# Token table of the second expert layer built sequence by sequence, and the first unit prepared norm first

## The chip, the cores and the metric

The kernel runs on one core of one Trainium2 chip. The metric is the time of one execution on the device in microseconds (us), taken as the median of several runs. Engines are named as in the profile: PE (matmuls), PEld (its weight loads), DVE (vector), ACT (scalar/activation), POOL (GpSimd), SP (the queue that issues most DMAs).

## The reference, cut to what matters

Two layers over `x` of shape (8, 256, 256): eight sequences of 256 tokens, width 256. Each layer is cross attention with 16 heads to a context of 256 tokens, added to `x`, and then a mixture of experts, added to `x`.

```python
x = x + tanh(g_xattn[0]) * L0_xattn(layernorm(x), ctx)      # layer 0
x = x + tanh(g_ffn[0])   * L0_ffn(layernorm(x))             # 8 experts (dense here) + a shared one
x = x + tanh(g_xattn[1]) * L1_xattn(layernorm(x), ctx)      # layer 1
x = x + tanh(g_ffn[1])   * L1_ffn(layernorm(x))             # 8 experts of 1024, each token to its top 2
# L1_ffn:
logits = x @ Wr + br;  mask = top-2 of the 8 logits;  w = softmax(logits where mask)
for e in range(8):
    out += (relu(x @ W1[e] + b1[e]) @ W2[e] + b2[e]) * (w * mask)[:, :, e]
```

## The kernel before, in words

**Units and slots.** A unit is one sequence of one layer: units 0 to 7 are layer 0, 8 to 15 layer 1. Every engine walks the same list of slots `PLAN` (made by `make_plan`), and in each slot it runs, in the order in which the list holds them, its own part of the stages named there. `base(u)` = 18 + 8u; a slot number here is a half step, so unit `u` starts its scores at slot 2*base(u). Waits between engines are semaphores; nothing reorders an engine's list at run time.

**Preparing a unit.** `ctx` turns the context (PE, then ACT), `kprod` makes the keys and `qprod` the queries (PE, then ACT writes a high part and DVE a low part), `stats`, `normal`, `turn` make the normed and turned `x` that `qprod` wants. SP stores keys and queries to DRAM and `load_stacks` brings them back stacked (`stack_k`, six DMAs; `stack_q`, six DMAs). `stats` is two steps on DVE (`bn_stats`, `bn_aggr`) and then eight tiny operations on POOL that make the inverse deviation `rstd` (L1702 to L1709). ACT then writes the normed rows (`normal`, L1020), PE turns them (`turn`, L655). For unit 0 the order is ctx, kprod, stats, normal, turn, qprod, stack.

**Scores.** `scores_by_query` (PE, L678) and `maxima` (DVE, L1243), `scores_by_key` (L699), exponentials on ACT, `weigh_values` (L714), `turn_values`, `attn_turn`, `project` (L741).

**Routing of layer 1.** For each sequence `b`, when its layer-1 attention is in: `pick_z` (DVE, and the add to `x` on POOL, L1724; for b = 7 on DVE), `stats` of ("finish", b), `normal`, `turn`, `logits1` (PE, L817; DVE ranks the eight logits and writes `mask` and `picks`), `soft1`, `count1` (PE: triangular and all-ones products of the masks, which give each token its place among the tokens of its expert), `weights1` (DVE, ending in L1475), a store of the rows, and `bias_turn` (L842) and `bias1` (L850), which add the expert bias and finish `x`. Before, `count1` writes into one array of all 16 tiles of tokens (`by_query`), and for b = 1 to 4 it stands at slots 294 to 297.

**After the last sequence.** `blocks` (DVE) turns the eight totals into 23 blocks of 256 slots, each of one expert. `tables` (DVE) then works on all 4096 picks at once: slot numbers, their tile and place, a 128x32x46 one-hot of the tile (`in_tile`, `in_tile_no`) and a 128x32x128 one-hot of the place (`at_place`, L1542, in four quarters); 32 matmuls (L881) make of them the token number of each slot, DVE makes `token_i` (L1589 to L1596). POOL gathers the rows by `token_i` (L1740), and the expert loop over the 23 blocks runs: `up` (L915), `down` (L931), scatter-add (L1753).

**What stands ahead of the expert loop.** PE: the b1 product (L888, after all eight `x` are finished), `turn_rows(0)` (L899), then `up(0)`. ACT: `split_w1(0)` (L1123), the copy `b1_all` (L1164), `split_w1(1)`, `split_rows(0)`. DVE: `split_w1(0)` (L1600), `split_w1(1)`, then `split_rows(0)` (L1611). SP: the store of the last rows, b1, then the first two blocks' W1 (`first_weights`).

Of the kernel before, what the change touches and what calls it, by code (L numbers as in the profile page):

```python
# [37 lines left out]
PICKS = TOPK1 * NT  # L38
# [22 lines left out]

def layer_of(u):
    return u // NB
# [11 lines left out]
def make_plan():  # L75

    at = defaultdict(list)
    for u in range(UNITS):
        g = 2 * base(u)
        at[g - 34].append(("load", u))  # L80
        at[g - 28].append(("ctx", u))
        at[g - 25].append(("kprod", u))
        at[g - 23].append(("stats", ("query", u)))
        at[g - 21].append(("normal", ("query", u)))
        at[g - 19].append(("turn", ("query", u)))
        at[g - 16].append(("qprod", u))
        at[g - 10].append(("stack", u))
# [9 lines left out]
    at[2 * base(0)].append(("out_bias", 0))  # L97
    at[2 * base(2)].append(("gate_turn", 0))
# [21 lines left out]
    for b in range(NB):  # L120
# [31 lines left out]
stats_done moments rstd rstd_chain norm_done turned xnT_ready  # L152
# [7 lines left out]
weights1_done rows_out0 rows_out1 rows_out2 rows_out3 biases_in b2_in table_chain in_tile_ready tile_no block_ready onehotT_ready b1_mm b1_ready  # L160
at_place_ready tokens_mm tokens_ready w1_in0 w1_in1 w2_in0 w2_in1 w1_hi w1_lo w2_hi w2_lo rows_in0 rows_in1 rows_in2 rows_in3 xs_turned
# [4 lines left out]
def bank_release(stage, n):  # L166

    if stage == "turn":
# [11 lines left out]
        "logits1": ("logits_ready", n + 1),  # L180
# [3 lines left out]
def share_banks():  # L184

    bank_of, uses = {}, []
    for g in sorted(PLAN):
        for stage, n in PLAN[g]:
            if stage in ("load", "stack", "stats", "normal", "take", "groups0", "ranks0", "weights0", "any_nan",
                         "reload", "load_alternative", "pick_z", "soft1", "count1", "weights1", "blocks", "tables") or (stage == "ctx" and layer_of(n)):  # L190
# [10 lines left out]
def build(nc, a, out):  # L201
# [40 lines left out]
    column_row = sb("column_row", [P, COLS])  # L242
# [4 lines left out]
    tile_start = sb("tile_start", [P, TOPK1 * NT])  # L247
    row_no = sb("row_no", [P, 1])
# [61 lines left out]

    b1 = sb("b1", [E1, H1])
# [3 lines left out]
    slots_all = sb("slots_all", [P, NT, E1])  # L315
    slots_pick = sb("slots_pick", [P, TOPK1, NT, E1])
    slot_f = sb("slot_f", [P, PICKS])
    slot_i = sb("slot_i", [P, 3, PICKS], I32)
    place_tile = sb("place_tile", [P, 2, PICKS])
    at_place = sb("at_place", [P, PICKS, P], BF16)  # L320
    in_tile = sb("in_tile", [P, PICKS, COLS])
    in_tile_no = sb("in_tile_no", [P, PICKS, 2, COLS], BF16)
# [6 lines left out]
    tok = sb("tok", [P, 3, COLS])  # L329
# [54 lines left out]
    def _(sp):  # L384
# [9 lines left out]
        def load_attention_weights(l):  # L394
            if l == 0:
                q_w, q_b, o_w, o_b = a["L0_xattn_q_w"], a["L0_xattn_q_b"], a["L0_xattn_proj_w"], a["L0_xattn_proj_b"]
                k_w, v_w = a["L0_xattn_kv_w"][:, 0:D], a["L0_xattn_kv_w"][:, D:2 * D]
                k_b, v_b = a["L0_xattn_kv_b"][0:D], a["L0_xattn_kv_b"][D:2 * D]
            else:
                q_w, q_b, o_w, o_b = a["L1_xattn_Wq"], a["L1_xattn_bq"], a["L1_xattn_Wo"], a["L1_xattn_bo"]  # L400
                k_w, v_w, k_b, v_b = a["L1_xattn_Wk"], a["L1_xattn_Wv"], a["L1_xattn_bk"], a["L1_xattn_bv"]
            for dst, src in (
                (wq[l][:, :, :], q_w.rearrange("(k p) n -> p k n", p=P)),
                (wkv[l][:, :, 0:D], k_w.rearrange("(k p) n -> p k n", p=CROWS)),
# [5 lines left out]
            for dst, col in ((qkb[l][:, 0, :], q_b), (qkb[l][:, 1, :], k_b), (vb[l][:, :], v_b)):  # L410
                sp.dma_start(dst, col.rearrange("(k p) -> p k", p=P),
                             allow_slow_non_contiguous=True).then_inc(attn_w_in[l], 16)
# [12 lines left out]
        def load_router():  # L425
            sp.dma_start(wr[:, :, :], a["L1_ffn_Wr"].rearrange("(k p) e -> p k e", p=P)).then_inc(sem.router_in, 16)
            sp.dma_start(br[:, :], a["L1_ffn_br"].partition_broadcast(P)).then_inc(sem.router_in, 16)
            sp.dma_start(b2[:, :], a["L1_ffn_b2"]).then_inc(sem.b2_in, 16)
# [50 lines left out]
        def load_stacks(u):  # L479
# [5 lines left out]
            for blk in range(PARTS):  # L485
                src = qk_dram[l][b, 2 + blk % 2].rearrange("(h two d) s -> two d h s", two=2, d=HD)
                for side in range(2):
                    o = HALF * side + blk * HD
                    sp.dma_start(stack_k[i][o:o + HD, :, :].bitcast(F32), src[side]).then_inc(k_in[i], 16)
            sp.wait_ge(sem.q_out, 32 * (u + 1))  # L490
# [74 lines left out]
        def store_rows(b):  # L565
            sp.wait_ge(sem.weights1_done, b + 1)
# [3 lines left out]
        sp.dma_start(g_raw[:, 0:2], a["g_xattn"].partition_broadcast(P)).then_inc(sem.gates_in, 16)  # L570
        sp.dma_start(g_raw[:, 2:4], a["g_ffn"].partition_broadcast(P)).then_inc(sem.gates_in, 16)
        load_x(0)
        load_ctx(0)
        stages = {"load": load, "ctx": context, "kprod": store_keys, "qprod": store_queries, "stack": load_stacks,
                  "shift_turn": place_shift, "mean_project": store_alternative, "project": store_z, "reload": reload, "load_alternative": load_alternative,
                  "weights1": store_rows, "bias1": store_x, "tables": first_weights}
# [17 lines left out]
    def _(pe):  # L594
# [215 lines left out]
        def logits1(b):  # L810
            no = NORM_NO["finish", b]
            bank = open_bank("logits1", b)
            pe.wait_ge(sem.router_in, 32)
# [7 lines left out]
        def count1(b):  # L821
# [954 lines left out]
```

## Time and profile before

| what | value |
|---|---|
| median of 3 runs | 1077.18 us (1073.37 to 1077.26) |
| the profiled execution's own time | 1083.7 us |
| its span, first to last instruction | 1081.9 us |
| PE busy | 943.0 us, 87% |
| DVE busy | 757.0 us, 70% |
| ACT busy | 479.5 us, 44% |
| POOL busy | 222.6 us, 21% |
| mean granted TensorE clock | 0.890 of full speed |
| expert loop, from the first `up` (792.65) to the end | 289.3 us |

The profiled execution is 6.5 us (0.6%) above the median of the timed ones. Shares of busy time are means over stages with different limits, so they are only a start: what a change in one stage is worth is read from the rows of that stage.

### The profile page before, as it was taken

The numbers are of one execution on the slowest core, as the hardware profiler recorded it, in microseconds if no ns is written. First come the engines' busy times: TensorE is split into PE (matmuls) and PEld (weight loads), VectorE is DVE, ScalarE is ACT, GpSimd is POOL, SyncE is SP. The second block draws the span as 40 slices with busy tenths as digits, with TensorE's granted clock in tenths as the row PEclk, the third lists the DMA queues.
The fourth block names the chain that finished last, engine by engine and source line by source line (L and its number), as shares of the span: only waits on it lengthen the run. The fifth ranks groups of instructions, "written<-read, shape, count | busy, mean of one in ns | idle before, by whom it ended". The sixth has DMA issues, their size and how long they took to land.

```text
span 1081.9 us, 17951 instructions
## 1 busy us (share of the span) xinstructions
PE 943.0 (87%) x6385; PEld 745.0 (69%) x6385; DVE 757.0 (70%) x1553; ACT 479.5 (44%) x834; POOL 222.6 (21%) x386
## 2 busy tenths in 40 slices
PE   3478899999999998899888868897479999999995
PEld 2345677777777665666655545564379999999995
DVE  2544475777676667788786688865668888888882
ACT  1115544344444442333423343442256667666762
POOL 2011210120201000000000012201044454445423
PEclk9756899999999998999989776655579999999998
DMA  4997563353262316366353873241257677667752
GB/s 117 203 224 151 108 124 61 52 106 69 50 100 54 62 61 110 87 109 139 83 108 94 157 202 96 87 122 42 108 197 243 197 231 235 217 202 233 236 152 29
DMA packets 121336, 142.16 MB, mean 131 GB/s; under 512 B 11456, under 2 KB 105560, under 8 KB 121120
## 3 DMA queue, kind: packets, MB, share of 16 engines
q1 hardware_dynamic: 112416, 128.77, 47.5%
q0 software_dynamic: 8832, 12.25, 5.2%
q8 instruction: 51, 0.84, 0.3%
q14 instruction: 37, 0.30, 0.1%
HBM read 109.97 MB, written 31.01 MB: 130 GB/s over the span
## 4 chain that ended last, share of the span: by engine, by line
PE 62%; DVE 20%; issue 7%; ACT 5%; DMA 3%; POOL 2%; SPq 1%; DVEq 0%; POOLq 0%; ACTq 0%
PE bank L931 12%; PE bank L770 7%; PE by_query L915 6%; PE by_key L915 6%; DVE rowmax L1243 5%; PE value_bank L714 4%; PE bank L780 4%; DVE clipped L1268 4%; PE bank L741 3%; PE by_query L678 3%; PE bank L634 3%; PE bank L625 3%; PE by_key L699 2%; PE bank L664 2%; DVE x L1398 1%
## 5 line engine op out<-in xcount | busy, mean ns | idle before, releaser
L1243 DVE TENSOR_REDUCE rowmax<-by_query 128x4 f32<-128x1024 f32 x128 | 155.7, 1217 | 26.6 <-PE by_query L678 26.4
L1057 ACT ACTIVATE probs<-clipped 128x1024 f32<-128x1024 f32 x64 | 67.6, 1057 | 183.7 <-DVE clipped L1268 183.7
L1702 POOL TENSOR_SCALAR rstd<-moments 128x2 f32<-128x2 f32 x32 | 7.1, 223 | 579.5 <-DVE moments L1207 579.5
L1753 POOL DMA_INDIRECT out_x<-x,token_i x46 | 78.2, 1700 | 146.5 <-ACT x L1158 139.5
L931 PE MATMUL bank<-w_hi,h_hi 128*128 128x256 f32 x368 | 104.1, 283 | 0.0
L931 PE MATMUL bank<-w_lo,h_hi 128*128 128x256 f32 x368 | 104.1, 283 | 0.0
L931 PE MATMUL bank<-w_hi,h_lo 128*128 128x256 f32 x368 | 104.1, 283 | 0.0
L678 PE MATMUL by_query<-stack_k,stack_q 48*128 48x256 f32 x512 | 70.9, 358 | 28.7 <-DVE rowmax L1243 23.2
L1268 DVE SCALAR_TENSOR_TENSOR clipped<-by_key,lower 128x512 f32<-128x512 f32 x128 | 82.0, 682 | 13.2 <-DMA lower<-max 11.1
L678 PEld LDWEIGHTS by_query<-stack_k,stack_q 48*128 48x128 f32 x512 | 43.2, 208 | 68.3 <-issue 35.5
L699 PE MATMUL by_key<-stack_q,stack_k 50*128 50x256 f32 x512 | 68.1, 348 | 19.6 <-DVE clipped L1268 15.6
L770 PE MATMUL bank<-xnT,w_gate 128*128 128x256 f32 x288 | 79.5, 399 | 5.5 <-DVE lo L1224 2.2
L780 PE MATMUL bank<-w_down,hidden 128*128 128x256 f32 x288 | 79.2, 398 | 4.6 <-DVE hidden L1384 1.5
L714 PE MATMUL value_bank<-probs,values 128*32 128x256 f32 x1024 | 80.4, 439 | 0.0
L699 PEld LDWEIGHTS by_key<-stack_q,stack_k 50*128 50x128 f32 x512 | 43.7, 209 | 48.3 <-issue 23.3
L770 PE MATMUL bank<-xnT,w_up 128*128 128x256 f32 x288 | 75.7, 386 | 0.0
L1398 DVE SCALAR_TENSOR_TENSOR x<-bank,expert_cols,x 128x256 f32<-128x256 f32 x144 | 62.5, 476 | 17.9 <-PE bank L780 17.8
L1090 ACT ACTIVATE act_gate<-bank 128x256 f32<-128x256 f32 x72 | 27.4, 380 | 103.8 <-PE bank L770 103.8
L1057 ACT ACTIVATE probs<-by_key 128x1024 f32<-128x1024 f32 x64 | 65.4, 1022 | 16.8 <-PE by_key L699 15.3
L931 PEld LDWEIGHTS bank<-w_hi,h_hi 128*128 128x128 f32 x368 | 70.7, 192 | 0.0
L931 PEld LDWEIGHTS bank<-w_lo,h_hi 128*128 128x128 f32 x368 | 70.7, 192 | 0.0
L931 PEld LDWEIGHTS bank<-w_hi,h_lo 128*128 128x128 f32 x368 | 70.7, 192 | 0.0
(230 smaller groups left out, 2215.7 us busy)
## 6 DMA issues: line engine op xcount, KB each, us to landing
w<-in_L_ffn_W SPq DMA_DIRECT2D x46, 1024.0 KB, 8.8
lower<-max SPq DMA_DIRECT2D x64, 256.0 KB, 3.5
stack_k<-qk SPq DMA_DIRECT2D x96, 128.0 KB, 4.7
stack_q<-qk SPq DMA_DIRECT2D x96, 128.0 KB, 7.2
qk<-hi SPq DMA_DIRECT2D x32, 256.0 KB, 3.5
qk<-lo SPq DMA_DIRECT2D x32, 256.0 KB, 4.3
rows<-w_gate SPq DMA_DIRECT2D x8, 264.0 KB, 3.8
x<-in_x SPq DMA_DIRECT2D x8, 256.0 KB, 6.9
```

Of the source, the lines that this page charges most:

```text
L678: mm = pe.matmul(by_query[:, side, t * S:t * S + S], sq[rows, p, t * P:t * P + P], sk[rows, p, :], start=True, stop=True)
L699: mm = pe.matmul(by_key[:, side, kt * S:kt * S + S], sk[rows, p, kt * P:kt * P + P], sq[rows, p, :], start=True, stop=True)
L714: mm = pe.matmul(value_bank[32 * c:32 * c + 32, o:o + S], values[u % 2][:, kt, 4 * j + c, :], probs[(i + c // 2) % 4][:, c % 2, kt, :], st ...
L770: mm = pe.matmul(bank[:, half * S:half * S + S], w[:, k, e, :], turned_of(("ffn0", b))[:, k, :], start=k == 0, stop=k == 1)
L780: mm = pe.matmul(bank[:, t * D:t * D + D], hidden0[i % 6][:, t * P:t * P + P], w_down0[:, e, :], start=True, stop=True)
L915: mm = pe.matmul(up_bank[pair][:, half * SLOTS:half * SLOTS + SLOTS], wt[:, k, j * P:j * P + P], xt[:, k, :], start=n == 0, stop=n == len( ...
L931: mm = pe.matmul(bank[:, t * D:t * D + D], ht[:, j, t * P:t * P + P], wt[:, j, :], start=j == 0 and t == 0 and n == 0, stop=j == JH - 1 an ...
L1057: ac.activation(probs[i % 4][:, :, :, :].rearrange("p h k s -> p (h k s)"), src, ACT.Exp).then_inc(sem.exp_done, 1)
L1243: dv.tensor_reduce(rowmax[u % 2][:, 2 * p:2 * p + 2, :], by_query[:, :, :].rearrange("p h (t s) -> p h t s", t=TT), AX, ALU.max).then_inc( ...
L1268: op = dv.scalar_tensor_tensor(clipped[i % 2][:, side, :, :], by_key[:, side, :].rearrange("p (k s) -> p k s", k=2), 0.0, lower[j % 2][:, ...
L1398: op = dv.scalar_tensor_tensor(xt, bank[:, t * D:t * D + D], expert_cols[b % 2][:, t, e:e + 1], xt, ALU.mult, ALU.add)
L1753: po.indirect_dma_start(out[:, :], bass.IndirectOffsetOnAxis(ap=token_i[:, n:n + 1].bitcast(U32), axis=0), ysb[i % 3][:, t, :], None, comp ...
```

## The change

It has two parts.

1. **The token table is built as each sequence is routed.** `count1(b)` now gives only the places of sequence `b`'s two tiles, with the masks of the earlier sequences summed on POOL (`mask_sum`). A new stage `places(b)`, for b = 0 to 6, copies the ranks from PSUM on ACT and works out, on POOL, key = expert * 2048 + rank for the four (pick, tile) pairs, its place within 128 and its table entry, and then eight one-hots of 128x128 (four `at_entry`, four `at_place` scaled by the token number). `table(b)` (PE) adds four products of them into a 128x128 table in PSUM. The last sequence does the same on DVE (`last_places`). At the end ACT copies the table, `select` (DVE) makes a 128x46 one-hot of the entries that the blocks use, and one matmul (`tokens`) picks the columns. `count1` moves to slots 293, 298, 303, 308, 313, 318, 323, 332; `places(b)` stands one slot behind `count1(b)`, `table(b)` at 302, 307, 312, 317, 322, 327, 331. `bias_turn` and `bias1` of the last sequence go behind `tokens` (slots 340 and 342, before 335 and 337). The last store of rows moves from SP's queue to ACT's, and SP loads the first weights right behind `blocks`.

2. **Unit 0 is prepared norm first** (`FIRST`): stats, ctx, normal, scaling of the query weights, turn, kprod, load of `stack_k`, qprod, load of `stack_q`. The stack load is split in two stages. Five small loads of the start (three biases, two gates) move from SP's queue to ACT's; `wk` is loaded ahead of `wq`; ACT no longer waits for the attention weights and PE no longer for all constants; the fill of `values` on DVE moves behind the fills of `stack_k`.

In the list of slots, slot 324 holds `places(6)`, `bias_turn(6)` and `stats(("finish", 7))` in this order, and slot 294 `places(0)` and `stats(("finish", 5))`.

```diff
+FIRST = [("stats", ("query", 0)), ("ctx", 0), ("normal", ("query", 0)), ("scale_queries", 0), ("turn", ("query", 0)),
+         ("kprod", 0), ("stack_keys", 0), ("qprod", 0), ("stack_queries", 0)]
...
-        at[max(g + 10, 2 * base(UNITS) + 1 + b)].append(("count1", b))
-        if b == NB - 1:
-            at[g + 11].append(("blocks", 0))
-            at[g + 12].append(("tables", 0))
-        at[g + 11].append(("weights1", b))
-        late = 5 if b == NB - 2 else 0
+        counting = max(g + 10, 2 * base(UNITS) + 1 + 5 * b)
+        at[counting].append(("count1", b))
+        if b < NB - 1:
+            at[counting + 1].append(("places", b))
+            at[min(counting + 9, 2 * base(UNITS) + 39)].append(("table", b))
+        else:
+            for i, stage in enumerate(("blocks", "weights1", "last_places", "table", "select", "tokens")):
+                at[g + 11 + i].append((stage, b))
+        if b < NB - 1:
+            at[g + 11].append(("weights1", b))
+        late = 5 if b >= NB - 2 else 0
...
         def count1(b):
+            else:
+                pe.wait_ge(sem.ranks_read, b)
+                pe.wait_ge(sem.places_ready, PLACES * (b - 1) + 1)
...
+        def table(b):
+            if b < NB - 1:
+                pe.wait_ge(sem.places_ready, PLACES * (b + 1))
+            else:
+                pe.wait_ge(sem.last_places, 2 * NOW)
+            for j in range(NOW):
+                mm = pe.matmul(by_query[:, 1, 0:P], at_entry[b % 2][:, j, :], at_place[b % 2][:, j, :],
+                               start=b == 0 and j == 0, stop=b == NB - 1 and j == NOW - 1, skip_group_check=True)
+            mm.then_inc(sem.placed, 1)
...
-            for q in range(4):
-                part = slice(q * quarter, (q + 1) * quarter)
-                dv.tensor_tensor(at_place[:, part, :], place_tile[:, 0, part].unsqueeze(2).broadcast_to([P, quarter, P]),
-                                 place_row[:, :].unsqueeze(1).broadcast_to([P, quarter, P]), ALU.is_equal).then_inc(
-                    sem.at_place_ready, 1)
...
+        def select(_):
+            table(dv.tensor_tensor(ended[:, :, :], ended[:, :, :], c(2).unsqueeze(1).broadcast_to([P, BLOCKS, E1]), ALU.mult))
+            tabled()
+            table(dv.tensor_reduce(block_shift[:, :], ended[:, :, :], AX, ALU.add))
+            tabled()
+            dv.scalar_tensor_tensor(selected[:, :, :], block_shift[:, :].unsqueeze(2).broadcast_to([P, BLOCKS, BT]), -1.0,
+                                    column_less_part[:, :, :], ALU.mult, ALU.is_equal).then_inc(sem.onehots_ready, 1)
...
+        def places(b):
+
+            tiles, half, keys = slice(TT * b, TT * b + TT), b % 2, keys2[b % 2]
+            if b >= 2:
+                po.wait_ge(sem.placed, b - 1)
+            po.wait_ge(sem.counted, b + 1)
+            now = mask[:, TT * b, :]
+            if b:
+                chained(po.tensor_tensor(mask_sum[:, :], mask_sum[:, :], now, ALU.add))
+                now = mask_sum[:, :]
+            po.tensor_tensor(mask_sum[:, :], now, mask[:, TT * b + 1, :], ALU.add).then_inc(sem.places_ready, 1)
+            po.wait_ge(sem.ranks_read, b + 1)
+            chained(po.tensor_tensor(keys[:, 0, :, :], keys[:, 0, :, :], table_row[:, :].unsqueeze(1).broadcast_to([P, TT, E1]),
+                                     ALU.add))
+            po.wait_ge(sem.picks_ready, TOPK1 * (b + 1))
+            chained(po.tensor_tensor(keys[:, 1:1 + TOPK1, :, :], picks[:, :, tiles, :],
+                                     keys[:, 0:1, :, :].broadcast_to([P, TOPK1, TT, E1]), ALU.mult))
+            picked = keys[:, 1:1 + TOPK1, :, :].rearrange("p r t e -> p (r t) e")
+            chained(po.tensor_tensor(picked[:, :, 0:4], picked[:, :, 0:4], picked[:, :, 4:8], ALU.add))
+            chained(po.tensor_tensor(picked[:, :, 0:2], picked[:, :, 0:2], picked[:, :, 2:4], ALU.add))
+            chained(po.tensor_tensor(key_f[:, :], picked[:, :, 0], picked[:, :, 1], ALU.add))
+            chained(po.tensor_scalar(key_parts[:, 0, :], key_f[:, :], 1.0 / P, 0.5 / P - 0.5, ALU.mult, ALU.add))
+            chained(po.tensor_scalar(key_parts[:, 0, :], key_parts[:, 0, :], WHOLE, None, ALU.add))
+            chained(po.tensor_scalar(key_parts[:, 1, :], key_parts[:, 0, :], -WHOLE, None, ALU.add))
+            chained(po.tensor_scalar(key_parts[:, 0, :], key_parts[:, 1, :], -float(P), None, ALU.mult))
+            chained(po.tensor_tensor(key_parts[:, 0, :], key_parts[:, 0, :], key_f[:, :], ALU.add))
+            for j in range(NOW):
+                no = TT * b + j % TT
+                po.tensor_scalar(at_entry[half][:, j, :], place_row[:, :], key_parts[:, 1, j:j + 1], None,
+                                 ALU.is_equal).then_inc(sem.places_ready, 1)
+                po.tensor_scalar(at_place[half][:, j, :], place_row[:, :], key_parts[:, 0, j:j + 1], token_no[:, no:no + 1],
+                                 ALU.is_equal, ALU.mult).then_inc(sem.places_ready, 1)
```

## Rows read from the trace of the kernel before

**Rows 1.** Chain that ended last, first 130 us: start, length, what.
```profile
6.23 5.06 DMA vb<-in_L_xattn_kv_b
...
12.29 3.77 PE bank L625 x8
...
36.48 8.47 DMA stack_q<-qk
```

**Rows 2.** DMA issues of the first 60 us: count, size, median us to landing.
```profile
qk<-lo SPq DMA_DIRECT2D x4, 256.0 KB, 4.1
...
stack_q<-qk SPq DMA_DIRECT2D x6, 128.0 KB, 7.6
```

**Rows 3.** Timeline of the first 40 us: start, us, engine.
```profile
6.11 0.14 POOL L1686 IOTA row_no<- 128x1 f32 x1
...
31.29 2.78 SPq L489 DMA_DIRECT2D stack_k<-qk  x6
...
34.11 2.80 SPq L495 DMA_DIRECT2D stack_q<-qk  x6
```

**Rows 4.** Timeline, start of unit 1.
```profile
63.62 0.44 SPq L495 DMA_DIRECT2D stack_q<-qk  x1
...
72.57 0.80 PE L678 MATMUL by_query<-stack_k,stack_q 48*128 48x256 f32 x4 [1.42 <-DVE rowmax L1243]
```

**Rows 5.** Groups of POOL's instructions by shape: total us, mean ns of one.
```profile
L1724 POOL TENSOR_TENSOR x<-x,w_up 128x512 f32<-128x512 f32 x7 | 8.9, 1269 | 70.2 <-DVE w_up L1432 70.2
L1702 POOL TENSOR_SCALAR rstd<-moments 128x2 f32<-128x2 f32 x32 | 7.1, 223 | 579.5 <-DVE moments L1207 579.5
...
L1708 POOL TENSOR_TENSOR rstd<-rstd 128x2 f32<-128x2 f32 x32 | 6.3, 198 | 2.7
...
L1663 POOL TENSOR_SCALAR_AFFINE_SELECT tri<-tri 128x128 bf16<-128x128 bf16 x1 | 0.3, 292 | 0.1
```

**Rows 6.** Timeline, 703 to 713 us, first count and rstd of sequence 5.
```profile
703.48 0.21 PE L827 MATMUL by_query<-mask,tri 128*128 128x8 bf16 x1
...
706.45 0.22 POOL L1702 TENSOR_SCALAR rstd<-moments 128x2 f32<-128x2 f32 x1 [2.92 <-DVE moments L1207]
...
708.93 0.19 POOL L1709 TENSOR_TENSOR rstd<-rstd 128x2 f32<-128x2 f32 x1
...
712.71 1.10 PE L655 MATMUL bank<-ident,w_gate 128*128 128x128 f32 x4
```

**Rows 7.** Timeline, 738 to 758 us, from rstd of sequence 6 to that of 7.
```profile
738.24 0.19 POOL L1709 TENSOR_TENSOR rstd<-rstd 128x2 f32<-128x2 f32 x1
...
750.25 3.75 PE L741 MATMUL bank<-wo,attnT 128*128 128x256 f32 x8 [0.84 <-ACT attnT L1071]
...
757.84 0.22 POOL L1702 TENSOR_SCALAR rstd<-moments 128x2 f32<-128x2 f32 x1 [19.41 <-DVE moments L1207]
```

**Rows 8.** Timeline, from the last weights to the first expert product.
```profile
771.38 0.23 DVE L1475 SCALAR_TENSOR_TENSOR w_gate<-route,tg 128x16 f32<-128x16 f32 x1
...
772.96 2.04 PE L850 MATMUL bank<-b,wT 8*128 8x256 f32 x4 [0.61 <-ACT wT L1000]
...
776.84 4.62 DVE L1542 TENSOR_TENSOR at_place<-place_tile,place_row 128x1024 bf16<-128x1024 f32 x4
...
782.38 3.60 PE L888 MATMUL bank<-onehotT,b 8*128 8x23 f32 x16
...
783.13 0.21 DVE L1596 TENSOR_TENSOR token_i<-tok 128x46 int32<-128x46 f32 x1
...
786.24 1.90 ACT L1123 ACTIVATE w_hi<-w 128x2048 fp32r<-128x2048 f32 x1
...
788.17 2.29 DVE L1600 TENSOR_TENSOR w_lo<-w,w_hi 128x2048 fp32r<-128x2048 f32 x1 [2.29 <-ACT w_hi L1123]
...
791.90 0.69 DVE L1611 TENSOR_TENSOR xs_lo<-value_bank,xs_hi 128x512 fp32r<-128x512 f32 x1 [1.44 <-ACT xs_hi L1135]
...
792.65 0.58 PE L915 MATMUL by_query<-xs_hi,w_hi 128*128 128x256 f32 x1 [1.41 <-DVE xs_lo L1611]
```

More of the change, by code:

```diff
@@ L80, in make_plan @@
         at[g - 34].append(("load", u))
[L81 to L87, printed above, removed]
+        if u == 0:
+            for i, stage in enumerate(FIRST):
+                at[g - 30 + i].append(stage)
+        else:
+            at[g - 28].append(("ctx", u))
+            at[g - 25].append(("kprod", u))
+            at[g - 23].append(("stats", ("query", u)))
+            at[g - 21].append(("normal", ("query", u)))
+            at[g - 19].append(("turn", ("query", u)))
+            at[g - 16].append(("qprod", u))
+            at[g - 10].append(("stack_keys", u))
+            at[g - 10].append(("stack_queries", u))
         at[g + 13].append(("vprod", u))
@@ L188, in share_banks @@
         for stage, n in PLAN[g]:
-            if stage in ("load", "stack", "stats", "normal", "take", "groups0", "ranks0", "weights0", "any_nan",
-                         "reload", "load_alternative", "pick_z", "soft1", "count1", "weights1", "blocks", "tables") or (stage == "ctx" and layer_of(n)):
+            if stage in ("load", "stack_keys", "stack_queries", "stats", "scale_queries", "normal", "take", "groups0", "ranks0", "weights0", "any_nan",
+                         "reload", "load_alternative", "pick_z", "soft1", "count1", "weights1", "blocks", "places", "last_places", "table", "select") or (stage == "ctx" and layer_of(n)):
                 continue
@@ L309, in build @@
     first.close()
+    at_entry = [sb(f"at_entry{i}", [P, NOW, P]) for i in range(2)]
+    at_place = [sb(f"at_place{i}", [P, NOW, P]) for i in range(2)]
     b1 = sb("b1", [E1, H1])
@@ L1545, in tables, with tokens @@
             table(dv.tensor_tensor(onehot[:, :, :], expert_row[:, :].unsqueeze(1).broadcast_to([P, BLOCKS, E1]),
                                    block_e[:, :].unsqueeze(2).broadcast_to([P, BLOCKS, E1]), ALU.is_equal))
+        def tokens(_):
+            found = banks[BANK_OF["tokens", NB - 1][0]][:, 0:COLS].rearrange("p (i t) -> p i t", t=BT)
+            dv.wait_ge(sem.tokens_mm, 1)
+            for t in range(BT):
+                table(dv.tensor_scalar(unused_row[:, :, t], found[:, :, t], 0.0, spare_row[:, t:t + 1], ALU.is_equal, ALU.mult))
+            tabled()
+            dv.scalar_tensor_tensor(token_i[:, :].rearrange("p (i t) -> p i t", t=BT), found, -1.0, unused_row[:, :, :],
+                                    ALU.add, ALU.add).then_inc(sem.tokens_ready, 1)
@@ L1570, in _ @@
                     fill_ones(i)
+                for t in values:
+                    dv.memset(t[:, :, :, HD:2 * HD], 1.0)
+                dv.wait_ge(sem.const, 1)
             v, q = divmod(g - base(0), PAIRS)
@@ L1673, in _ @@
         triangle(before[:, :, :], 8, [[1, 8], [-1, 8]], 0)
+        made_const(po.memset(upto[:, :, :], 1.0))
+        made_const(po.affine_select(out=upto[:, :, :], in_=upto[:, :, :], compare_op=ALU.is_ge, fill=0.0, base=0,
+                                    pattern=[[1, E1], [-1, E1]], channel_multiplier=0))
         triangle(tri[:, :], P, [[1, P]], -1)
@@ L1727, in _ @@
+        stages = {"stats": stats, "vprod": add_out_bias, "pick_z": pick_z, "places": places}
         for f in range(2 * SLOTS_IN_ALL):
```

245 lines of the change are left out of this document (129 added, 116 removed).

## The prediction

> **What bounds the kernel now.** I read the page first: PE is busy 87% of the span, and the chain that ended last runs through PE for 62% and DVE for 20%. So only stages in which that chain leaves a busy PE can give something. I then read the chain in order of time, the timeline of the two stretches that the change touches, and the groups by shape for prices.
>
> At the start nothing is bound by arithmetic. The chain waits until 11.3 us for small bias loads issued last on SP's queue [rows 1], then makes keys, norm and queries of unit 0 one after the other on an almost empty PE, and ends in a wait for the stacked queries: SP issues six `stack_k` loads and six `stack_q` loads [rows 3], and the last of these lands 8.47 us after its issue, at 44.95 [rows 1]. The first score product starts at 45.1.
>
> From there to about 735 us PE and DVE carry the chain. Between 738 and 793 the routing of sequences 6 and 7 is a chain of small steps on all engines, with PE mostly idle. `rstd` of sequence 7 starts as soon as its moments are there, at 757.84 [rows 7]. From the last weights (771.6) DVE works for 11.7 us until `token_i` is ready at 783.34, of which `at_place` alone is 4.6; 9.3 us later, through gather, turn and split, the first `up` starts at 792.65 [rows 8]. The expert loop behind it is one unbroken PE chain of 289.3 us that the change doesn't touch.
>
> **The change, part by part.** I work against the profiled execution (1083.7 us) and move the sum to the median at the end.
>
> *Head: -4.7.* The bias loads go first on ACT's queue, so they stop mattering. POOL's constants end at 6.25 now [rows 3]; with the net of the added and removed ones I put them at 7.0. `rstd` takes 2.7 from first start to last end [rows 6], so 9.65; normed rows 1.1, turn 1.1 (four transposes, [rows 6]) gives 11.95. `kprod` 3.77 [rows 1] ends at 15.7, its low part is stored from 17.55, `k_out` lands 4.1 later [rows 2] at 21.7. Here a new order counts: `stack_keys` stands ahead of the query stores in SP's list, so SP issues six loads (2.8, [rows 3]) before it stores queries that have been ready since 21.2. They go out at 24.6 and 25.0, land at 29.1; six `stack_q` issues end at 31.95, against 36.91 now: 4.95 earlier. The landing of the last one, 7.6 to 8.5 [rows 1, 2], puts the first score product at 39 to 40, 5 to 6 earlier. DVE isn't in the way: its four fills of `stack_k` and the moved fill of `values` end at about 38. But SP then still owes x, context and context store of the next unit (1.5), which before went out ahead of the stacks, so `stack_q` of unit 1 is only 3.45 earlier. Today that load lands about 71.7 (issue at 63.62 plus 0.43 and 7.6) and the first product that needs it runs at 72.57 [rows 2, 4]: 0.9 of slack, so some 4.4 to 5 survive. I take 4.7; ends 2 (a later DMA wait binds) and 7 (landing in 6.3, slack all used).
>
> *PE in 703 to 735: +1.5.* The counts cost the same as before. New are four 128x128 products for each `table`. The nearest row is four transposes of the same size in 1.10 [rows 6], half of that at full clock. `table(0)` and `table(1)` lie where PE carries the chain: 2 x 0.55 to 1.1, I take 1.5. Later tables stand in front of waits that are longer: nothing.
>
> *The price P of one `places` on POOL.* It has 12 small dependent or near-small operations and 8 of 128 elements. Small ones cost 0.20 to 0.22 each plus 0.08 until the next may start [rows 5]; with up to 32 elements in two of them the twelve make 3.45. For a 128-element `tensor_scalar` with pointers no row exists. From below: the affine select of the same size, 0.29. From above: the two-input rate, (1.269 - 0.198)/510 = 2.1 ns an element, so 0.20 + 0.27 = 0.47 [rows 5]. It reads one large input, so I stand nearer the first: 0.33, with 0.07 between, 0.40, times 8 = 3.2. So P = 6.65; ends: 3.45 + 8 x 0.26 = 5.5 (if the fixed part alone were paid), and 3.45 + 8 x 0.54 = 7.8.
>
> The Trainium skill (GPSIMD Engine Reference, 3.1 and 4.1) speaks against elementwise work there: about 2.6 cycles of 1.2 GHz an element with two inputs, roughly one with one input. By its first figure a 128-element operation would be 0.48 and P about 7.85; by its second 0.31 and P about 6.5. The two-input row here, 2.1 ns, agrees with 2.6 cycles; no row shows the one-input case.
>
> *What queues behind `places` on POOL.* POOL runs its list in order, and `rstd` is on it.
> - Sequence 5: `places(0)` waits for the count at about 703.95, is one operation shorter, and ends at 710.35. `rstd(5)`, which now starts at 706.45, follows it and ends at 713.05; normal adds 1.1, so the turn that now starts at 712.71 starts at 714.15 [rows 6]: +1.4.
> - Sequence 7: `rstd(6)` ends at 738.43 [rows 7]. Behind it stand `places(3)`, (4), (5), (6), then `rstd(7)`. Their counts (PE at about 734, 741, 748 and, behind `project` which ends at 754.0, at 755) come no later than POOL can take them, so the four run back to back: 738.45 + 4 x 6.65 = 765.05 in place of 757.84 [rows 7]: +7.2. Everything behind it is late: norm, turn, logits, count, blocks. Even with a free POOL `places(6)` can't start before 755.1, so this can't fall below 755.1 + P.
>
> *Tail: -3.4.* In the clock of the trace before. `blocks` loses a copy and one step, 0.4, so the last weights are ready at 771.2. `last_places`: six short steps 1.35; eight DVE operations of 128 elements at 0.22 (a quarter of `at_place`, 1024 elements, is 1.155 [rows 8]: 0.133 for 128 plus 0.09) 1.8, to 774.3; four products 1.1; table copy 0.4; one product 0.45; three short DVE steps 0.7: `token_i` at 777.0, 6.3 earlier. By the 9.3 behind it `up` would start at 786.3. But another path is next: `bias_turn` now waits behind `tokens`, 776.3; `bias1` 1.2 later and 2.04 long, the add 0.75, the b1 product 3.60 [rows 8], 783.95. Behind it ACT's `b1_all` and `w_hi(1)`, DVE's `w_lo(1)`, then `xs_lo`: now 785.98 to 790.46 and 0.75 more, 5.25, so `up` at 789.2. W1, whose load starts 2 earlier, is there. 792.65 - 789.2 = 3.4; ends 2.5 and 6.3 (the path of the gather alone).
>
> *Sum:* -4.7 + 1.5 + 1.4 + 7.2 - 3.4 = +2.0. On 1083.7 that is 1085.7; the profiled execution stands 6.5 above the median, so the median goes from 1077.2 to 1079.2. The difference of 0.2% is inside the 0.5% that a measurement of this kernel can tell from no change.
>
> **Rivals.**
> - *POOL is quick (0.30).* P = 5.5, the fixed cost alone. Then +0.3 for sequence 5 and 738.45 + 22 = 760.45, +2.6, for 7: the sum is -3.7, 1073.5; with the head at -7 it is 1071.2. For: the 128-element memset and affine select are barely dearer than tiny ones. Against: they don't compare or read pointers.
> - *POOL is slow: the other side (0.22).* P = 7.8, because compares with pointer operands go at the two-input rate. +2.6 and 738.45 + 31.2 = 769.65, +11.8: sum +7.8, 1085.0. It is slower by over 0.5% from P = 7.35 on, since the sum moves by 5 us for 1 us of P.
> - *The head gives nothing (0.08).* A wait for SP or a transfer between units 1 and 3 sets the pace, and the earlier start is waited out: +4.7, 1083.9. For: the experts' weights, 12 DMAs, stand in SP's list behind unit 0. Against: the slack of 0.9 and the PE chain behind 73 us.
> - *As summed (0.40).* 1079.2, own range 1075 to 1083.
>
> **From these to the numbers.** Range 1069 to 1086: from the quick POOL with head and tail at their ends, to the slow POOL. Faster by over 0.5% (below 1071.8): two thirds of the quick case and some of the likeliest with a better tail, 0.27. Slower (above 1082.6): most of the slow case, the headless one, a little of the likeliest, 0.28. Within: 0.45.
>
> **What would show each step.** First L678 product at 39 to 40. POOL's `places` at 6.4 long, with 8 operations of about 0.33. Between `rstd(6)` and `rstd(7)` no pause on POOL, and the latter about 7 behind its moments, which stay at 757.7 less the head. `token_i` about 6 after the last weights, the first `up` about 18 after them (now 21.0), bound by `w_lo(1)` and not by the gather. It is wrong if the 128-element operations cost far from 0.33, or if POOL shows pauses between `places(3)` and (6), so that the backlog I work with isn't there.

## The result, and the profile after

The changed kernel takes 1092.76 us (median of 6 runs, 1089.56 to 1097.29) against 1075.42 for the kernel before (6 runs, 1071.07 to 1077.26): ratio 1.0167, 95% interval 1.0136 to 1.0197. It is slower by 17.3 us. The forecast was 1079.2, its range ended at 1086.

The profiled execution of the changed kernel took 1097.29 us, 4.5 above its median, with a span of 1095.6. Line numbers moved: `rstd` is L1769 to L1776, the one-hots of `places` are L1821 and L1823, `x` plus `z` on POOL is L1791, the scores are L705 and L726, the turn is L682, the logits are L844, the table products L877, the bias products L900, the b1 product L931, the first `up` L958.

The page's line for the engines and the chain that ended last:

```profile
PE 945.4 (86%) x6413; PEld 752.6 (69%) x6413; DVE 750.5 (69%) x1554; ACT 479.3 (44%) x841; POOL 280.8 (26%) x527
...
PE 56%; DVE 16%; POOL 7%; issue 7%; DMA 5%; ACT 4%; SPq 4%; ACTq 0%; POOLq 0%; DVEq 0%
```

POOL works 58 us more than before (222.6), and its part of the chain grew from 2% to 7%. POOL's groups by shape say with what (total us, mean ns of one, idle before):

```profile
L1823 POOL TENSOR_SCALAR at_place<-place_row,key_parts,token_no 128x128 f32<-128x128 f32 x28 | 22.6, 808 | 0.0
L1821 POOL TENSOR_SCALAR at_entry<-place_row,key_parts 128x128 f32<-128x128 f32 x28 | 17.3, 619 | 0.8
```

A one-hot costs 0.62 or 0.81 us, not 0.33. The timeline from `rstd` of sequence 6 to that of 7 answers to [rows 7] (start, us, engine):

```profile
735.79 0.24 POOL L1769 TENSOR_SCALAR rstd<-moments 128x2 f32<-128x2 f32 x1 [1.23 <-DVE moments L1270]
...
738.47 0.20 POOL L1801 TENSOR_TENSOR mask_sum<-mask_sum,mask 128x8 bf16<-128x8 bf16 x1
...
747.70 0.20 POOL L1801 TENSOR_TENSOR mask_sum<-mask_sum,mask 128x8 bf16<-128x8 bf16 x1
...
756.60 0.43 POOL L1801 TENSOR_TENSOR mask_sum<-mask_sum,mask 128x8 bf16<-128x8 bf16 x1
...
766.15 0.21 POOL L1801 TENSOR_TENSOR mask_sum<-mask_sum,mask 128x8 bf16<-128x8 bf16 x1
...
775.07 0.24 POOL L1769 TENSOR_SCALAR rstd<-moments 128x2 f32<-128x2 f32 x1
```

Four `places` stand back to back, none with a bracket for idle time before it, 36.60 us for the four: 9.15 each on the mean, 8.90 to 9.55 singly. The moments of sequence 7 are ready at 759.19, and `rstd` starts 15.9 us after them. Before, it started with them.

There are two more places where PE stands still for POOL. They answer to [rows 6] and to a stretch that the prediction didn't look at (a bracket is the idle time of that engine and what ended it):

```profile
695.59 0.20 POOL L1803 TENSOR_TENSOR mask_sum<-mask 128x8 bf16<-128x8 bf16 x1 [0.30 <-PE by_query L866]
...
697.80 0.25 DVE L1270 BATCH_NORM_AGGREGATE moments<-stats 128x2 f32<-128x6 f32 x2
...
706.30 0.24 POOL L1769 TENSOR_SCALAR rstd<-moments 128x2 f32<-128x2 f32 x1
...
709.12 1.09 ACT L1063 ACTIVATE w_gate<-x,rstd 128x256 f32<-128x256 f32 x2 [7.35 <-POOL rstd L1776]
...
710.36 1.09 PE L682 MATMUL bank<-ident,w_gate 128*128 128x128 f32 x4 [5.80 <-ACT w_gate L1063]
...
733.29 1.26 POOL L1791 TENSOR_TENSOR x<-x,w_up 128x512 f32<-128x512 f32 x1
734.59 0.75 DVE L1266 BATCH_NORM_STATS2 stats<-x 128x6 f32<-128x256 f32 x2 [3.80 <-POOL x L1791]
...
735.54 1.25 DVE L1331 SCALAR_TENSOR_TENSOR clipped<-by_key,lower 128x512 f32<-128x512 f32 x2
...
736.85 0.80 PE L726 MATMUL by_key<-stack_q,stack_k 50*128 50x256 f32 x4 [5.26 <-DVE clipped L1331]
```

First, `places(0)` holds `rstd` of sequence 5 until 706.30, and PE waits 5.80 for the turn. Then `places(2)`, which starts right behind `places(1)` at 724.17, holds the add that makes `x` of sequence 6, for which DVE is ready at 728.00. DVE's statistics wait for that add, the clip of the attention stands behind them in DVE's list, and PE waits 5.26 for the clip. Of the 10.71 that `places(0)` takes, 1.68 is a wait for ACT's copy of the ranks:

```profile
697.47 0.22 POOL L1805 TENSOR_TENSOR keys<-keys,table_row 128x16 f32<-128x16 f32 x1 [1.68 <-ACT keys L1155]
```

The tail answers to [rows 8]:

```profile
788.27 0.23 DVE L1539 SCALAR_TENSOR_TENSOR w_gate<-route,tg 128x16 f32<-128x16 f32 x1
...
791.70 2.08 PE L877 MATMUL by_query<-at_place,at_entry 128*128 128x128 f32 x8 [6.39 <-DVE at_place L1602]
...
795.29 0.21 DVE L1621 SCALAR_TENSOR_TENSOR token_i<-bank,unused_row 128x46 int32<-128x46 f32 x1
...
795.87 2.04 PE L900 MATMUL bank<-b,wT 8*128 8x256 f32 x4 [0.61 <-ACT wT L1043]
...
798.76 3.61 PE L931 MATMUL bank<-onehotT,b 8*128 8x23 f32 x16 [0.85 <-DVE x L1505]
...
804.56 2.30 DVE L1664 TENSOR_TENSOR w_lo<-w,w_hi 128x2048 fp32r<-128x2048 f32 x1 [3.65 <-ACT w_hi L1186]
...
807.51 0.58 PE L958 MATMUL by_query<-xs_hi,w_hi 128*128 128x256 f32 x1 [3.35 <-DVE xs_lo L1675]
```

The first `up` comes 19.0 us after the last weights are ready (788.5), where it was 21.0. The table's four products appear as eight matmuls and take 2.08 here, not 1.1.

### The profile page after: what moved, and what is told of

The parts are those of the page before. It is cut to its first block, busy times and chain, and to the rows that moved or that the text cites. A ratio compares the mean times of both kernels' runs of the same rounds, so it can differ in the third digit from the quotient of the medians.

```text
span 1095.6 us, 18194 instructions
## 1 busy us (share of the span) xinstructions
PE 945.4 (86%) x6413; PEld 752.6 (69%) x6413; DVE 750.5 (69%) x1554; ACT 479.3 (44%) x841; POOL 280.8 (26%) x527
## 4 chain that ended last, share of the span: by engine, by line
PE 56%; DVE 16%; POOL 7%; issue 7%; DMA 5%; ACT 4%; SPq 4%; ACTq 0%; POOLq 0%; DVEq 0%
PE bank L974 12%; PE bank L797 8%; PE by_query L958 6%; PE by_key L958 6%; PE bank L807 4%; DVE rowmax L1306 4%; DVE clipped L1331 3%; PE value_bank L741 3%; PE by_query L705 2%; PE by_key L726 2%; PE bank L652 2%; PE bank L768 2%; POOL at_place L1823 2%; PE bank L661 2%; POOL at_entry L1821 2%
## 5 line engine op out<-in xcount | busy, mean ns | idle before, releaser
L1769 POOL TENSOR_SCALAR rstd<-moments 128x2 f32<-128x2 f32 x32 | 7.4, 230 | 546.3 <-DVE moments L1270 546.3
L705 PE MATMUL by_query<-stack_k,stack_q 48*128 48x256 f32 x512 | 71.9, 363 | 29.8 <-DVE rowmax L1306 22.0
L705 PEld LDWEIGHTS by_query<-stack_k,stack_q 48*128 48x128 f32 x512 | 43.9, 211 | 70.3 <-issue 39.1
L726 PE MATMUL by_key<-stack_q,stack_k 50*128 50x256 f32 x512 | 67.7, 346 | 25.4 <-DVE clipped L1331 19.8
L726 PEld LDWEIGHTS by_key<-stack_q,stack_k 50*128 50x128 f32 x512 | 43.6, 209 | 53.0 <-issue 23.3
L1133 ACT ACTIVATE act_gate<-bank 128x256 f32<-128x256 f32 x72 | 27.5, 382 | 103.9 <-PE bank L797 103.9
L974 PEld LDWEIGHTS bank<-w_hi,h_hi 128*128 128x128 f32 x368 | 70.7, 192 | 0.0
L974 PEld LDWEIGHTS bank<-w_lo,h_hi 128*128 128x128 f32 x368 | 70.7, 192 | 0.0
L974 PEld LDWEIGHTS bank<-w_hi,h_lo 128*128 128x128 f32 x368 | 70.7, 192 | 0.0
```

The lines of the kernel that those rows point to most:

```text
L705: mm = pe.matmul(by_query[:, side, t * S:t * S + S], sq[rows, p, t * P:t * P + P], sk[rows, p, :], start=True, stop=True)
L726: mm = pe.matmul(by_key[:, side, kt * S:kt * S + S], sk[rows, p, kt * P:kt * P + P], sq[rows, p, :], start=True, stop=True)
L974: mm = pe.matmul(bank[:, t * D:t * D + D], ht[:, j, t * P:t * P + P], wt[:, j, :], start=j == 0 and t == 0 and n == 0, stop=j == JH - 1 an ...
```

## The experiments

The medians below stand beside the median of the kernel before on the same chip in the same job: 1075.28 in the first four, 1076.75 in the next four, 1075.30 for `e9` and `e10`, 1077.27 for `e11` and `e12`. `e4` and `e5` were run once each, for their traces.

**e1: the new head alone.** The second part of the change on the old routing.

> The kernel before with the new head alone (unit 0 norm first, bias loads on ACT's queue, stacks in two halves), routing as before. The trace of the kernel after has its first score product 8.1 us earlier, and units 1 to 9 start 8.5 to 8.8 earlier, so the sum of my revised theory is -8 to -9 us against before, carried to the end. The prediction's own term was -4.7. Rival: a wait for the loads or for SP takes part of it back in the second layer, 0 to -4.

Measured: 1072.02, ratio 0.9967 (0.9942 to 0.9993), so -3.3. The first score product is 8.1 earlier, as in the changed kernel. The trace's span is 9.1 shorter than that of before, the median only 3.3: my figure of 8 to 9 was read from traces and was wrong. Against a second trace of before (`e5`, below) this one is only 1.0 shorter.

**e2: the routing with the old order of unit 0.** The changed kernel with unit 0's stages at the offsets of all other units (`at[g - 28].append(("ctx", u))` and so on). The moved small loads and the dropped waits of the start stay, so it isn't quite the routing alone: its first score product comes at 42.95, 2.1 ahead of before.

> The changed kernel with the stages of unit 0 in their old order, so that the queries are stored and stacked about as late as before. The theory that head and routing add up says: slower than the kernel after by about 8, so about +25 us against before, unless the head's gain is already lost there to the POOL backlog in the routing, whose start hangs on rstd of sequence 6 (735.8 in both traces): then about +17 and equal to the kernel after.

Measured: 1096.54, ratio 1.0183 (1.0148 to 1.0219), so +21.3, between the two. The changed kernel is at +17.3, so the new order is worth 4.0 there, and the whole head 3.3 in `e1`. Within intervals of some 3 to 4 us each way, the parts add up.

**e3: the one-hots on DVE.**

```diff
+            at[counting + 4].append(("hots", b))
...
+        def hots(b):
+            half, key_parts = b % 2, key_parts2[b % 2]
+            dv.wait_ge(sem.places_ready, PLACES * (b + 1))
+            if b >= 2:
+                dv.wait_ge(sem.placed, b - 1)
+            for j in range(NOW):
+                no = TT * b + j % TT
+                dv.tensor_scalar(at_entry[half][:, j, :], place_row[:, :], key_parts[:, 1, j:j + 1], None,
+                                 ALU.is_equal).then_inc(sem.last_places, 1)
...
-            for j in range(NOW):
-                no = TT * b + j % TT
-                po.tensor_scalar(at_entry[half][:, j, :], place_row[:, :], key_parts[:, 1, j:j + 1], None,
-                                 ALU.is_equal).then_inc(sem.places_ready, 1)
```

> The changed kernel, but the eight 128-element one-hots of each sequence are built on DVE, a few slots after POOL's small operations. Theory (the one-hots on POOL at 0.62 and 0.81 us make the backlog): places on POOL falls from 9.15 to about 3.5, four of them end at 752.5, before the moments of sequence 7, so rstd of sequence 7 starts with its moments at about 758 and not at 775: 17 us faster than the kernel after, about equal to before or up to 8 faster where the head's gain stays. DVE takes 8 x 0.22 = 1.8 us for each sequence in exchange. Rival (POOL's twelve small chained steps and the waits for the counts make the backlog): rstd of sequence 7 stays within 5 us of 775. Second rival: DVE, which carries the chain, now waits for POOL's parts, and the time is lost there.

Measured: 1074.78, ratio 0.999 (0.997 to 1.001): the loss against before is gone. The one-hots on POOL are the cause, not the small steps, which stayed there. Next to `e1` (-3.3) the kernel is still 2.8 behind, by intervals that overlap. The backlog is gone too: between `rstd` of 6 and of 7 POOL now waits 4.56 us for a count, where the changed kernel had no pause at all.

```profile
741.38 0.27 POOL L1811 TENSOR_TENSOR mask_sum<-mask_sum,mask 128x8 bf16<-128x8 bf16 x1 [4.56 <-PE by_query L867]
...
751.84 0.25 DVE L1268 BATCH_NORM_AGGREGATE moments<-stats 128x2 f32<-128x6 f32 x2
...
752.53 0.23 POOL L1779 TENSOR_SCALAR rstd<-moments 128x2 f32<-128x2 f32 x1
```

`rstd` of 7 starts 0.4 after its moments are ready (752.09). The second rival holds a little: the step that ends the moments of 7 starts 8.8 after the project of unit 15, not 7.2 as in the traces of before and after, and one-hots of earlier sequences stand ahead of it on DVE.

**e4: what a 128-element operation costs on POOL.** In the kernel before, three of each kind at POOL's start.

```diff
+        for _ in range(3):
+            chained(po.tensor_scalar(d[:, 0:128], place_row[:, :], 5.0, None, ALU.mult))
...
+            chained(po.tensor_scalar(d[:, 0:128], place_row[:, :], pt, qt, ALU.is_equal, ALU.mult))
```

> The kernel before with eight kinds of POOL operations, three of each, at POOL's start while DVE does next to nothing: 128 elements with an immediate (multiply; compare; compare and multiply), the same three with pointer operands, a compare of 4 elements with a pointer, and a two-input multiply of 128. If the compare is what costs, the compare with an immediate is 0.6 us too; if the pointer operand is, the multiply with a pointer is 0.6; if it was DVE's company in the routing, all are near 0.3; if the second operation is the difference of 0.19 between 0.62 and 0.81, it shows with immediates too. The prediction's 0.33 holds if the multiply with an immediate is near it. Its total time says nothing: it holds about 12 us of extra POOL work at the start.

POOL's groups by shape. L1702: immediate multiply; L1704: immediate compare; L1706: both, immediates; L1708 and L1710: pointer multiply and compare; L1712: both, pointers; L1714: pointer compare of 4 elements; L1716: two inputs.

```profile
L1712 POOL TENSOR_SCALAR scratch<-place_row,spare_row,row_no 128x128 f32<-128x128 f32 x3 | 2.4, 788 | 0.3
L1706 POOL TENSOR_SCALAR scratch<-place_row 128x128 f32<-128x128 f32 x3 | 2.2, 736 | 0.2
L1708 POOL TENSOR_SCALAR scratch<-place_row,spare_row 128x128 f32<-128x128 f32 x3 | 1.8, 605 | 0.3
L1710 POOL TENSOR_SCALAR scratch<-place_row,spare_row 128x128 f32<-128x128 f32 x3 | 1.8, 602 | 0.3
L1702 POOL TENSOR_SCALAR scratch<-place_row 128x128 f32<-128x128 f32 x3 | 1.6, 540 | 0.3
L1704 POOL TENSOR_SCALAR scratch<-place_row 128x128 f32<-128x128 f32 x3 | 1.6, 531 | 0.2
...
L1716 POOL TENSOR_TENSOR scratch<-place_row,ones 128x128 f32<-128x128 f32 x3 | 1.4, 453 | 0.2
L1714 POOL TENSOR_SCALAR scratch<-place_row,spare_row 128x4 f32<-128x4 f32 x3 | 0.9, 293 | 0.3
```

It is none of the suspects alone. The plain multiply with an immediate already costs 0.54. The compare adds nothing, pointers add 0.06, the second operation adds 0.19. DVE did nothing while the first two kinds ran (6.3 to 10.0 us), and the prices are those of the routing within 0.02.

**e5: the kernel before once more, unchanged.**

> The kernel before, unchanged, profiled once more. The traces of the other kernels are up to 9 us shorter than the profiled execution of before, where their medians are 3.3 shorter or less. Theory: that execution of before waited some us longer for stack loads in its first 130 us than most do, so a second one has its sixth group of 16 score products (131.18 in the first trace) 2 to 4 us earlier, and a span near 1074. Rival: it is the same, and the medians differ from the traces for another reason.

Measured: 1075.59, span 1073.8. The theory holds in size, not in place: of the 8.0 us between the two executions of one kernel, at the project of unit 15, only 1.8 had arisen by 131 us, 3.6 by the project of unit 8 and 7.1 by that of unit 13. So a difference of two traces below some 8 us says nothing here about a change, unless it is read inside one stage.

**e6: one slot.** `places(6)` behind `stats(("finish", 7))`.

```diff
-            at[counting + 1].append(("places", b))
+            at[counting + (2 if b == NB - 2 else 1)].append(("places", b))
```

> The changed kernel with one slot changed: places of sequence 6 stands behind rstd of sequence 7 in POOL's list instead of ahead of it. Backlog theory: rstd of 7 starts at 738.45 + 3 x 9.15 = 765.9 in place of 775.1, and places(6) ends at about 778, still ahead of the last weights (about 779), so all of it is gained: 9 us faster than the kernel after, 8 slower than before. Rival: last_places and the last table, which need places(6), take its place in the wait: less than 4 of the 9 arrive.

Measured: 1086.96, ratio 1.0097 (1.0062 to 1.0133), so +10.2 against +17.3: about 7 of the 9, give or take 5 by the intervals. By stages less is due to the slot. From the project of unit 15 to the last logits it saves 8.2 (table below), and 3.8 of it comes back behind them, which leaves 4.4; another 2.2 (70.1 less 67.9) lies before the project of unit 15, where the edit changed nothing. So the rival holds in part, though by another wait than it named. The table of sequence 6 needs `places(6)`, and on PE it stands ahead of the count of sequence 7, for which `blocks` waits:

```profile
769.22 2.08 PE L877 MATMUL by_query<-at_place,at_entry 128*128 128x128 f32 x8 [3.91 <-POOL at_place L1823]
```


**e7 and e8: what is left of the tail.** `e7` is `e3` with `late = 5 if b == NB - 2 else 0`, which puts the bias products of sequence 7 ahead of the token lookup. `e8` also has the one-hots of 5 and 6 at slots 325 and 329.

> The kernel with the one-hots on DVE, and the expert biases of sequence 7 turned and added before the token lookup rather than after it. Theory: the tail is bound by b1 product, w_hi(1), w_lo(1), not by the gather; so the b1 product moves up by 1 to 3 us and the first up comes 23 us behind the last logits in place of 25.0, until the gather binds: about 2 us faster than the one-hots on DVE alone. Rival: the tail is bound by the gather and nothing comes of it, or DVE's add delays token_i by 0.75.

> As the one before, and the one-hots of sequences 5 and 6 stand in DVE's list where DVE waits anyway: behind the moments of sequence 7 and behind its turn. With them ahead, the moments of 7 came 8.9 us after the project of unit 15, in place of 7.3. Theory: 1.6 us come back, so it is some 3.5 us faster than the one-hots on DVE alone, and 2 faster than the new head alone with the old routing: about 1071. Rival: the wait moves to PE, whose table products of 5 and 6 now stand in front of the turn and the logits of 7, and nothing is gained.

Measured: `e7` 1070.46, ratio 0.9937 (0.9908 to 0.9967); `e8` 1072.08, ratio 0.9957 (0.9934 to 0.9981). The two can't be told apart by time; both beat the kernel before. In the trace of `e8` the b1 product ends early enough and the gather now binds, 9.5 from `token_i` to the first `up`:

```profile
769.45 3.61 PE L929 MATMUL bank<-onehotT,b 8*128 8x23 f32 x16 [0.26 <-DVE x L1503]
769.73 0.20 DVE L1631 SCALAR_TENSOR_TENSOR token_i<-bank,unused_row 128x46 int32<-128x46 f32 x1
...
776.73 1.12 PE L940 MATMUL value_bank<-ident,xs_in 128*128 128x128 f32 x4 [3.67 <-DMA xs_in<-rows,token_i]
```

Lengths of the stages, read from the starts of the same products in each trace (us; project 13 and 15 are those of units 13 and 15, the last logits are the last product of `logits1` for sequence 7):

| trace | project 13 to project 15 | to the last logits | to the first up | to the end |
|---|---|---|---|---|
| before | 61.2 | 15.0 | 27.4 | 289.3 |
| e5, before again | 60.2 | 15.0 | 27.4 | 289.2 |
| e1, new head | 59.8 | 15.0 | 27.5 | 289.1 |
| after | 70.1 | 30.8 | 25.0 | 288.0 |
| e2, old order of unit 0 | 70.7 | 30.4 | 25.0 | 288.7 |
| e6, one slot | 67.9 | 22.6 | 28.8 | 288.3 |
| e3, one-hots on DVE | 62.2 | 17.1 | 25.0 | 287.5 |
| e7 | 60.5 | 15.4 | 24.0 | 287.8 |
| e8 | 59.7 | 15.1 | 23.9 | 288.7 |

**e9 to e12: where the head's gain goes.** Only 3.3 of 8.1 us are left. `e9` is `e1` with the experts' loads moved behind unit 1's stacks on SP; in `e11` POOL issues them. `e10` and `e12` are the same on `e8`.

```diff
-            if u == 2:
-                load_experts0()
-            if u == 3:
+            if u == 6:
                 load_attention_weights(1)
...
+            if u == 1:
+                load_experts0()
```

> The new head with the old routing, and on SP's queue the 12 loads of the experts' weights moved behind the stack loads of unit 1, the weights of layer 1 from the load of unit 3 to that of unit 6. With the new head alone the first score product was 8.1 earlier, but by the fifth group of 16 only 2 to 6, and PE waited 3.7 for stack_q there; the stores of unit 1's queries stood on SP until 47.5 behind those 12 loads, which take it from 35.2 to 47.5. Theory (SP's order eats the head's gain): unit 1 then has its stacks in time, the third group of 16 (72.57 before) stays 7.5 to 8.5 earlier, and the whole is 2 to 4 us faster than the new head alone, 5 to 7 faster than before. Rival (the transfers themselves are slow or something later takes the gain back): less than 1 us.

> The same two moves of loads in the kernel with the one-hots on DVE in its waits and the biases early. If the parts add up, it is 2 to 4 us faster than that kernel without them, near 1068.5, and beats both kernels of the case by more than 6 us.

> The new head with the old routing; the 12 loads of the experts' weights are issued by POOL right behind rstd of unit 1's queries, not by SP, and the weights of layer 1 wait on SP until the load of unit 6. With the loads behind unit 1's stacks on SP, unit 1 was on time (third group of 16 9.7 earlier), but PE then waited 7.8 us for the shift rows of unit 0, stored at 69.27 behind the 12 loads, and 7.3 for the stacks of unit 2. Theory (SP's time for issuing): with POOL issuing them the bytes come at about the same time as with the new head alone, but SP has 12 us more; the seventh group (131.18 before) is 8 or more earlier and the whole 3 to 5 us faster than the new head alone. Rival (the bytes: 16 DMA engines full of expert weights delay the stacks whoever issues them): the waits for stack_q stay, and it is equal to the new head alone.

> The same with the one-hots on DVE in its waits and the biases early. Without POOL issuing the experts' weights that kernel measured 1072.1 against 1076.75 of before; if SP's time was the limit it comes to about 1068, if the bytes were, it stays near 1071.

Measured: `e9` 1076.64, ratio 1.0001 (0.9976 to 1.0025); `e10` 1072.79, 0.9984 (0.9953 to 1.0014); `e11` 1074.22, 0.9956 (0.9931 to 0.998); `e12` 1076.41, 0.9987 (0.9963 to 1.0011). PE's waits for loads from 36 to 135 us (total, times, longest), for `e1`, then `e9`, then `e11`:

```profile
PE by_query L692 <- DMA stack_q<-qk: 11.4, 2, 7.7
PE by_key L713 <- DMA stack_q<-max: 2.0, 1, 2.0
```

```profile
PE by_key L713 <- DMA stack_q<-max: 7.8, 1, 7.8
PE by_query L692 <- DMA stack_q<-qk: 7.3, 1, 7.3
```

```profile
PE by_query L679 <- DMA stack_q<-qk: 14.8, 1, 14.8
```

The forecasts of the theory of SP's order fail, but these runs don't rule it out. In `e9` the first score product that needs unit 1's stacks, at 72.57 before, is 9.7 us early, more than the 7.5 to 8.5 expected, and PE gives it back in the next two waits. One of them is SP's order again. The store of unit 0's shift rows stood behind the 12 loads on SP, and PE waited 7.8 for what was loaded from it:

```profile
69.27 0.54 SPq L516 DMA_DIRECT2D max<-shiftT  x1
```

In `e11` POOL issued the loads 8 us sooner than SP had, from 27.0, so that they went out with unit 0's own stacks:

```profile
44.27 0.80 PE L679 MATMUL by_query<-stack_k,stack_q 48*128 48x256 f32 x4 [14.84 <-DMA stack_q<-qk]
```

The head's start gain is gone (44.27 against 45.08 before), yet the total is as good as with it: -3.1 against -3.3. Neither `e10` nor `e12` is faster than `e8`. An earlier first product isn't what the head's 3 us consist of. What they consist of, whether bytes or single late landings set the pace up to 131 us, and why `e9` lost them, stays open.

## Why the prediction was wrong

**The step that failed is the price P of one `places` on POOL.** It was put at 6.65, with an upper end of 7.8; it is 9.15. The twelve small operations were right (3.45 predicted; 738.47 to the first one-hot at 741.93 is 3.46). The eight of 128 elements were put at 0.40 each and cost 0.68 to 0.72 from one to the next. I bounded them from below by an affine select (0.29) and from above by the two-input rate (0.47, [rows 5]), and chose nearer the first because one large input is read. `e4` shows that the upper end was no upper end: one input with one operation costs 0.53 to 0.60 on POOL, more than two inputs (0.45), and the second operation 0.19 more. The lower end was misread too. The quick rival was backed by a 128-element memset "barely dearer than tiny ones", and the trace of before has it at twice the price:

```profile
L1670 POOL MEMSET ones<- 128x128 f32 x1 | 0.2, 204 | 0.1
...
L1672 POOL MEMSET minus_half<- 128x2 f32 x1 | 0.1, 100 | 0.1
```

With the measured price the prediction's own sum moves by 5 us for 1 us of P: 1079.2 + 5 x 2.5 = 1091.7, against 1092.76 measured. The nearness is partly luck, since a missed add (below) and smaller errors offset. The formula for sequence 7 gives 738.45 + 4 x 9.15 = 775.05, and `rstd` started at 775.07, +17.2 where +7.2 stood. This is less of a test than it looks. The 9.15 is read from the same four `places`, and that `rstd(6)` ended at the same time in both traces is chance: the changed kernel's trace was 7.4 ahead at the project of unit 13 and 1.5 behind at that of unit 15. What it shows is that the four stood back to back, as forecast. The test of the price is `e3`: the one-hots gone from POOL, the loss is gone. So the rival "POOL is slow" had the right mechanism, and even it was priced too low, by the same wrong bound.

The other terms, by their steps:
- *Sequence 5, +1.4.* Right chain, same wrong P: PE paused 5.8. The 1.68 that `places(0)` waited for ACT's copy of the ranks was in no term either.
- *What queues behind `places`.* The list was short by one: the add of `x` for sequence 6 stands on POOL as well, behind `places(1)` and `(2)`, and through DVE's order cost PE 5.3. The three kernels with the one-hots on POOL take 7.7 to 10.5 us more from project 13 to project 15 than `e5`; 2.9 was forecast for that stretch, and 5.4 would follow from the measured P. The small steps of `places(2)` ended at 727.71, before DVE was ready; its eight one-hots hold the add. The TensorE clock is no rival for this stretch, since the granted clock was higher in it (0.70 in the changed kernel, 0.62 in `e5`).
- *PE in 703 to 735, +1.5.* The two tables took 1.77 and 1.16, together 2.9 and more than thought, but with the one-hots off POOL (`e7`, `e8`) project 13 to project 15 is no longer than before. That isn't the same as a price of nothing: the granted clock there was 0.72 and 0.74, against 0.61 and 0.62 in the traces of before and `e5`, which may have hidden it. It is counted as nothing below only because the stretch as a whole shows nothing.
- *Head, -4.7.* Right in size (-3.3 in `e1`, -4.0 by `e2`), and for no good reason: the start came 8.1 earlier, not 5 to 6 (SP's issues of `stack_q` ended at 31.4 in `e1` and the first product came 5.6 later, where 31.95 and 7.6 to 8.5 stood), and the loss behind it was larger than the slack of 0.9 that I counted.
- *Tail, -3.4.* -2.4 (25.0 from the last logits, in place of 27.4), bound by b1 and `w_lo(1)` as said. The missing 1.0 is the size of the table's four products, 2.08 where 1.1 stood. With the biases first it is -3.4 to -3.5.

The misses in head (+1.4), tail (+1.0) and PE (-1.5) add up to 0.9 us; they had no part in the error. By stages, the changed kernel against `e5` and the head at its measured -3.3: -3.3 + 9.9 + 15.8 - 2.4 - 1.2 = +18.8, near the measured +17.3.

On the one-input case the prediction weighed the Trainium skill (GPSIMD Engine Reference, 4.1), which puts one-input work at about line rate; the prediction's estimate from it was 0.31 for 128 elements. `e4` doesn't agree: 0.53 with one operation. Its figure for two inputs (the same page, 3.1) gave an estimate of 0.48 and is near the measured 0.45.

## What to carry to other kernels

Work that is "off the critical path" on an in-order engine is priced by what stands behind it in that engine's list: here 5.7 us of one-hots for each of seven sequences came out as some 18 us (`e3` against the changed kernel), through `rstd` and one add. List every instruction of that engine in the stretch, not only the one that comes to mind, and every wait for another engine inside the new work. And a price without a row of the same form (inputs, operations, operands) is not bounded by rows of other forms; leave the range open on that side, or put the work where a row exists.

Two traces of one unchanged kernel differed by 8 us. Compare stage by stage, and take the totals from medians.

## What the hardware showed that I had not expected

- On POOL a `tensor_scalar` of 128 elements costs 0.53 to 0.60 us with one operation and 0.74 to 0.79 with two, a `tensor_tensor` 0.45. The number of inputs doesn't order them.
- The same one-hots cost 0.28 and 0.34 us on DVE and overlap there: eight take 1.9 us from the first start to the last end, against 5.5 to 5.8 on POOL.
- Four f32 products of 128x128 appear as eight matmuls and cost nearly twice as much as four turns of the same size. At a granted clock of 0.50 they took 2.08 us against 1.09 to 1.11, at 1.00 they took 1.16 against 0.66:

```profile
716.72 1.11 PE L751 MATMUL bank<-ident,weighted 128*128 128x128 f32 x4
...
721.82 0.66 PE L760 MATMUL bank<-ident,attn 128*128 128x128 f32 x4
...
727.77 1.16 PE L877 MATMUL by_query<-at_place,at_entry 128*128 128x128 f32 x8
...
756.70 2.08 PE L877 MATMUL by_query<-at_place,at_entry 128*128 128x128 f32 x8 [1.19 <-POOL at_place L1823]
```

- From project 13 to project 15 the granted TensorE clock was 0.61 to 0.66 in the five traces with the old routing (before, `e1`, `e5`, `e9`, `e11`) and 0.69 to 0.76 in the eight with the new one, with or without the one-hots on POOL. So `e7` and `e8` hold more matmuls there than before, and no more time. Why the clock was higher there, no run shows.
